# One layer of a graph network on one core: tile firsts looked up by one-hot products, x normalised by the scalar engine

## The reference

```
h    = relu(layernorm(x))                       # per node, no scale or offset
att  = sigmoid(h[src] @ Wa[:128] + h[dst] @ Wa[128:] + b_att)
msg  = (h[src] @ W_msg + b_msg) * att
agg  = segment_sum(msg, dst)
r, z, n = GRU gates of (agg, h);  h_new = (1 - z) * n + z * h
out  = x + gamma * (h_new - mean) * rsqrt(var + eps) + beta   # statistics over nodes
```

## Time and profile before

| | |
|---|---|
| median of 3 runs | 2263.29 us |
| the profiled execution | 2263.15 us, span 2261.4 us |
| PE, DVE, ACT, POOL busy | 91%, 89%, 88%, 74% of the span |
| last gather of the preparation starts on POOL | 162.91 us |
| first row gather (L774) | 164.16 us |
| `gate(0)` on ACT | 166.83 us |
| keys of half 1 copied, main gates on ACT | 191.39 us |

### The profile page before, as it was taken

One profiled execution on the slowest core, in us unless ns is written; L12 is line 12 of the kernel. 1 busy time (PEld: TensorE's weight loads), 2 busy tenths in 40 slices (PEclk: granted clock), 3 DMA queues, 4 the chain that ended last, 5 costly groups with the idle time before them and its releaser, 6 DMA issues.

```text
span 2261.4 us, 53825 instructions
## 1 busy us (share of the span) xinstructions
PE 2051.0 (91%) x18152; PEld 1986.7 (88%) x18152; DVE 2014.4 (89%) x4410; ACT 1995.5 (88%) x6980; POOL 1681.0 (74%) x1601
## 2 busy tenths in 40 slices
PE   3625999999999999999999999999999999999997
PEld 2514999999999999999999999999999999999986
DVE  5947899999999999999999999999999999999974
ACT  1359899999999999999999999999999999999943
POOL 5776777777777777777777777777777777777760
PEclk8765999999999999999999999999999999999998
DMA  9952222222223322222222222222223222323236
GB/s 148 268 150 64 56 60 60 60 61 62 61 60 61 63 60 63 62 63 57 61 62 62 61 61 60 63 59 61 63 60 63 59 62 59 63 60 64 59 112 224
DMA packets 171174, 171.65 MB, mean 76 GB/s; under 512 B 82872, under 2 KB 135146, under 8 KB 170770
## 3 DMA queue, kind: packets, MB, share of 16 engines
q0 software_dynamic: 50688, 104.63, 21.5%
q1 hardware_dynamic: 114564, 61.63, 10.8%
q10 hardware_dynamic: 5646, 1.93, 0.8%
HBM read 141.39 MB, written 26.66 MB: 74 GB/s over the span
## 4 chain that ended last, share of the span: by engine, by line
ACT 53%; PE 20%; DVE 15%; issue 8%; POOL 3%; DMA 2%; SPq 1%; DVEq 0%; ACTq 0%; POOLq 0%
ACT big L903 41%; PE ps L1444 11%; ACT gate_ring L899 9%; DVE big L1195 5%; PE ps L1429 3%; PE ps L1439 3%; POOL big L765 2%; DVE gate_ring L1179 2%; DMA big<-in_x_dram 1%; DVE key_hot L1165 1%; DVE lo_hot L1158 1%; PE ps L1450 1%; PE ps L1451 1%; ACT n_blk L908 1%; SPq L624 1%
## 5 line engine op out<-in xcount | busy, mean ns | idle before, releaser
L774 POOL DMA_INDIRECT row_ring<-node_table,set_idx x1480 | 1568.4, 1060 | 464.4 <-issue 331.5
L903 ACT ACTIVATE big<-set_score,big 128x128 f32<-128x128 f32 x5096 | 1632.6, 394 | 82.5 <-PE ps L1444 82.5
L1444 PE MATMUL ps<-big 128*128 128x128 f32 x10192 | 1445.6, 281 | 0.0
L1444 PEld LDWEIGHTS ps<-big 128*128 128x128 f32 x10192 | 1262.6, 193 | 0.0
L1195 DVE TENSOR_TENSOR big<-ps,big 128x784 f32<-128x784 f32 x832 | 803.3, 966 | 5.7 <-PE ps L1439 4.4
L1429 PE MATMUL ps<-gate_ring,row_ring 128*128 128x64 f32 x2960 | 535.3, 263 | 77.5 <-DVE gate_ring L1179 71.4
L1429 PEld LDWEIGHTS ps<-gate_ring,row_ring 128*128 128x128 f32 x2960 | 453.9, 194 | 124.2 <-DVE gate_ring L1179 110.0
L1179 DVE SCALAR_TENSOR_TENSOR gate_ring<-lane,set_rel,gate_ring 128x64 f32<-128x64 f32 x1480 | 414.5, 281 | 136.1 <-ACT gate_ring L899 130.5
L899 ACT ACTIVATE gate_ring<-set_win,row_ring 128x64 f32<-128x64 f32 x1480 | 492.2, 341 | 34.2 <-DMA row_ring<-node_table,set_idx 33.6
L1439 PE MATMUL ps<-key_hot,lo_hot 128*128 128x196 bf16 x3328 | 426.7, 251 | 28.7 <-DVE key_hot L1165 24.3
L1165 DVE TENSOR_TENSOR key_hot<-lane_key,set_key 128x1568 bf16<-128x1568 bf16 x416 | 402.7, 968 | 0.0
(11 more groups left out here) (124 smaller groups left out, 932.2 us busy)
## 6 DMA issues: line engine op xcount, KB each, us to landing
row_ring<-node_table,set_idx POOLq DMA_INDIRECT x1480
big<-in_x_dram SPq DMA_DIRECT2D x48, 256.0 KB, 5.7
h_blk<-hT_spill SPq DMA_DIRECT2D x97, 64.0 KB
node_table<-big SPq DMA_DIRECT2D x24, 258.0 KB
hT_spill<-big SPq DMA_DIRECT2D x24, 256.0 KB, 5.9
out_dram<-big SPq DMA_DIRECT2D x24, 256.0 KB
set_win<-dst_scores SPq DMA_DIRECT2D x148, 32.0 KB
set_score<-dst_scores SPq DMA_DIRECT2D x52, 64.0 KB
```

Of the source, the lines that this page charges most:

```text
L774: nc.gpsimd.indirect_dma_start(row_ring[:, t % ROWS_RING, :], None, table, bass.IndirectOffsetOnAxis(ap=set_idx[:, t // SET % 2, t % SET:t ...
L903: return nc.scalar.activation(a_buf[b % 2][:, h, :], set_score[:, b % 2, :], ACT.Sigmoid, bias=m_all[:, h, D:ROW])
L1444: return nc.tensor.matmul(ps[:, AM_BANK, 0:P], m_all[:, h, 0:D], a_buf[b % 2][:, h, :], start=h == 0, stop=h == HI - 1)
```

## The change

Three things are edited.

1. The search for tiles. `COARSE` becomes 125 and `FINE` 25. ACT loads all of dst (1.6 MB) into 125 partitions of 3200, and for each partition the first dst of the next one (124 elements); the DRAM table, its two element-wise copies, `find_rows` and the 26 gathers of L753 go. DVE cuts the first dst of each tile out of it (`find_starts`), makes for each half a mask of 125 x 1664 that is one where the query falls into the partition (two instructions), PE multiplies the mask with the 25 tile firsts and the number of the partition's first tile (13 products for a half, `read_starts`), and DVE counts in the product. That happens at c = 2 and 3, ahead of those passes' other work. POOL makes the line of 3328 queries by an `iota`.
2. The normalisation. z = x * rstd + shift on ACT with a scale and an offset for each row (four instructions for a chunk, in pass c for chunk c-1, behind the relu and the square root), with shift = -mean * rstd from DVE. DVE's four instructions of L1122 go. SP's load of x waits for z as before, which ACT now makes.
3. Places in the loop. `find_firsts` moves from c = 15 and 18 to c = 10 and 15, `sparse_windows` and ACT's cast from c = 5 to 8, the turning and copying of edges by three passes, the store of the sparse lists from c = 15 to 18.

```diff
-    COARSE = next(r for r in range(30, 0, -1) if TILES % r == 0)
+    COARSE = next(r for r in range(P, 0, -1) if TILES % r == 0)
...
@@ sync
-                if c == 15:
+                if c == 18:
                     sp.wait_ge(edges_kept, 8)
...
@@ gpsimd
+            nc.gpsimd.memset(row_next, float(NODES)).then_inc(q_line_made, 1)
+            nc.gpsimd.iota(starts[:, FINE:FINE + 1], [[0, 1]], base=0, channel_multiplier=FINE, ...
+            nc.gpsimd.iota(q_line, [[PAIR, QCOLS * P]], base=D0, channel_multiplier=0, ...
...
-            pool.wait_ge(starts_stored, 32)
-            pool.wait_ge(rows_found, 1)
-            for half in range(2):
-                rows = half_of(near, half, FINE)
-                for i, c in enumerate(HALVES[half]):
-                    nc.gpsimd.indirect_dma_start(rows[:, i, :], None, tile_starts, found(c)).then_inc(near_gathered[half], 16)
             for half in range(2):
                 rows = half_of(wins, half, P)
-                pool.wait_ge(near_gathered[half], 16 * len(HALVES[half]))
                 pool.wait_ge(tiles_found, half + 1)
@@ scalar
-                act.dma_start(coarse_i, ...), two act.dma_start into tile_starts
+            for rows in (slice(0, even_rows), slice(even_rows, COARSE)):
+                act.dma_start(dst_tiles[rows, :], tile_rows[rows, :]).then_inc(starts_loaded, 16)
+                for first, end in ((0, even_rows), (even_rows, COARSE - 1)):
+                    act.dma_start(next_i[first:end, :], tile_rows[first + 1:end + 1, 0:1]).then_inc(starts_loaded, 16)
...
+                if 0 <= c - 1 < CHUNKS:
+                    d, r = c - 1, (c - 1) % 2
+                    act.wait_ge(shift_done, d + 1)
+                    wait_reuse(act, z_turned, d - 1)
+                    for j, n in tiles_of(width_of(d)):
+                        last = nc.scalar.activation(zbuf[0:n, r, j, :], xbuf[0:n, d % 4, j, :], ACT.Identity,
+                                                    bias=shift[0:n, r, j:j + 1], scale=rstd[0:n, r, j:j + 1])
+                    last.then_inc(z_done, 1)
...
-                if c == 5:
+                if c == 8:
                     act.wait_ge(sparse_loaded, 64)
...
-                if 7 <= c < 17:
-                    keep_edges(c - 7)
+                if 10 <= c < 20:
+                    keep_edges(c - 10)
@@ vector
+            def find_starts():
+                dve.wait_ge(starts_loaded, 64)
+                dve.wait_ge(q_line_made, 3)
+                nc.vector.tensor_copy(starts[:, 0:FINE], dst_tiles.rearrange("r (f e) -> r f e", e=P)[:, :, 0])
+                link(nc.vector.tensor_copy(row_first, dst_tiles[:, 0:1]))
+                nc.vector.memset(row_first[0:1, :], -1.0)
+                link(nc.vector.tensor_copy(row_next[0:COARSE - 1, :], next_i[0:COARSE - 1, :]))
...
             def find_tiles(half):
-                dve.wait_ge(near_gathered[half], 16 * len(HALVES[half]))
-                cols = count_below(half, near[half], FINE)
+                cols, n = cols_of(half), len(HALVES[half])
+                queries, hot = q_line[:, half * QHALF * P:(half + 1) * QHALF * P], near[half][0:COARSE, :]
+                link(nc.vector.tensor_scalar(hot, queries, row_first, None, ALU.is_gt))
+                nc.vector.scalar_tensor_tensor(out=hot, in0=queries, scalar=row_next, in1=hot, op0=ALU.is_le, op1=ALU.mult
+                                               ).then_inc(tile_hots, 1)
+                dve.wait_ge(starts_read, half + 1)
+                rows = ps[:, 6 + half, 0:n * (FINE + 1)].rearrange("p (c f) -> p c f", f=FINE + 1)
+                below = grid(cmps, half, FINE)
+                link(nc.vector.tensor_tensor(below, rows[:, :, 0:FINE], at(q_at[:, cols], FINE), ALU.is_lt))
+                link(nc.vector.tensor_reduce(q_cnt[:, cols], below, AX_X, ALU.add))
                 link(nc.vector.tensor_scalar(q_tmp[:, cols], q_cnt[:, cols], -1.0, 0.0, ALU.add, ALU.max))
+                link(nc.vector.tensor_tensor(q_tile[:, cols], rows[:, :, FINE], q_tmp[:, cols], ALU.add))
                 nc.vector.tensor_copy(q_idx.bitcast(U32)[:, cols], q_tile[:, cols]).then_inc(tiles_found, 1)
...
-            find_rows()
             for c in range(CHUNKS + 3):
+                if c == 2:
+                    find_starts()
+                if c in (2, 3):
+                    find_tiles(c - 2)
                 if c < CHUNKS:
                     ...
+                    wait_reuse(dve, shift_done, c - 1)
...
-                    for j, n in tiles:
-                        last = nc.vector.tensor_scalar(zbuf[0:n, r, j, :], xbuf[0:n, d % 4, j, :],
-                                                       mv[0:n, r, j, 0:1], rstd[0:n, r, j:j + 1],
-                                                       ALU.subtract, ALU.mult)
-                    last.then_inc(z_done, 1)
+                    nc.vector.scalar_tensor_tensor(out=shift[:, r, 0:len(tiles)], in0=mv[:, r, 0:len(tiles), 0], scalar=-1.0,
+                                                   in1=rstd[:, r, 0:len(tiles)], op0=ALU.mult, op1=ALU.mult
+                                                   ).then_inc(shift_done, 1)
...
-                if c == 5:
+                if c == 8:
                     sparse_windows()
-                if c in (7, 11):
-                    find_tiles((c - 7) // 4)
-                if c in (15, 18):
-                    find_firsts((c - 15) // 3)
+                if c in (10, 15):
+                    find_firsts((c - 10) // 5)
@@ tensor
+            def read_starts(half):
+                pe.wait_ge(tile_hots, half + 1)
+                for i in range(len(HALVES[half])):
+                    last = nc.tensor.matmul(ps[:, 6 + half, i * (FINE + 1):(i + 1) * (FINE + 1)],
+                                            near[half][0:COARSE, i * P:(i + 1) * P], starts, start=True, stop=True)
+                last.then_inc(starts_read, 1)
...
             for c in range(CHUNKS + 2):
+                if c in (2, 3):
+                    read_starts(c - 2)
...
-                if 6 <= c < 16:
+                if 9 <= c < 19:
```

More of the change, by code:

```diff
@@ L159, in gnn_program @@
     assert SPARSE % SET == 0 and GROUPS % 2 == 0 and DENSE_AT + PARTS < STEPS_U + 4 and PARTS_AT + PARTS < STEPS_U and SETS > 2 and TILES % 16 == 5
+    assert QCOLS == 2 * QHALF and (FINE + 1) * QHALF <= 512 and FINE * P <= QCOLS * P
     assert B_FIRST < HI and first_tile(1) >= GATES_EARLY and ZEROED <= D0 and -(-STEPS // 5) <= WIN and all(
@@ L217, in gnn_program @@
         b_table = place(WIDE)
-        coarse_i = place(COARSE, 1).bitcast(I32)
-        coarse = place(COARSE, 1)
+        starts = place(FINE + 1, COARSE)
+        row_first = place(1, COARSE)
+        row_next = place(1, COARSE)
+        next_i = place(1, COARSE).bitcast(I32)
         assert spot[0] <= LN_AT + (HI - 10) * P
@@ L226, in gnn_program @@
         wins = [place(QHALF * P) for _ in range(2)]
+        dst_tiles = part(spot[0] - 2 * QHALF * P, FINE * P, COARSE).bitcast(I32)
         cmps = place(QHALF * P)
@@ L234, in gnn_program @@
         key_out = [place(QHALF * P) for _ in range(2)]
+        q_line = part(spot[0] - 2 * QHALF * P, 2 * QHALF * P, COARSE)
         b_turned = [place(P, rows) for rows in (B_FIRST, HI - B_FIRST)]
@@ L239, in gnn_program @@
         rstd = place(8).rearrange("p (b t) -> p b t", b=2)
+        shift = place(8).rearrange("p (b t) -> p b t", b=2)
         q_at = place(QCOLS)
-        q_row = place(QCOLS)
         q_tile = place(QCOLS)
@@ L350, in gnn_program @@
         rstd_done = sem("rstd_done")
+        shift_done = sem("shift_done")
         z_done = sem("z_done")
@@ L737, in _ @@
                                     pattern=[[1, P]], channel_multiplier=-1).then_inc(consts_made, 1)
+            nc.gpsimd.memset(row_next, float(NODES)).then_inc(q_line_made, 1)
+            nc.gpsimd.iota(starts[:, FINE:FINE + 1], [[0, 1]], base=0, channel_multiplier=FINE,
+                           allow_small_or_imprecise_dtypes=True).then_inc(q_line_made, 1)
+            nc.gpsimd.iota(q_line, [[PAIR, QCOLS * P]], base=D0, channel_multiplier=0,
+                           allow_small_or_imprecise_dtypes=True).then_inc(q_line_made, 1)
             def found(c):
@@ L836, in cast_lo @@
                 nc.scalar.copy(near[half][:, cols], near[half].bitcast(I32)[:, cols]).then_inc(lo_cast, 1)
-            with nc.allow_non_contiguous_dma(reason="one destination per tile of edges"):
-                act.dma_start(coarse_i, dst.rearrange("(o r e) -> o r e", o=1, r=COARSE)[:, :, 0]).then_inc(coarse_loaded, 16)
-                starts = dst.rearrange("(t e) -> t e", e=P)[:, 0]
-                stored = tile_starts.rearrange("r f -> (r f)")
-                act.dma_start(stored[TILES - 5:TILES].rearrange("(o n) -> o n", o=1),
-                              starts[TILES - 5:TILES].rearrange("(o n) -> o n", o=1)).then_inc(starts_stored, 16)
```

(9 more changed lines are left out.)

34 lines of the change are left out of this document (8 added, 26 removed).

## The result

Over 20 runs of each, the changed kernel takes 2266.93 us (2260.43 to 2273.82) and the kernel before 2264.31 us (2260.43 to 2267.84); the ratio is 1.0017 [1.001, 1.0025]. That is 3.9 us slower by the ratio, within 0.3%, where 8 us faster was forecast. The profiled execution took 2269.91 us, span 2268.2. The engines' shares of the whole span are within 2 points of those before (ACT 88 to 90%, DVE 89 to 88%).

The account below looks back on a forecast made before the run. POOL's gathers bound the kernel, the loop 10.6 us early; after the change the longer loop decides, gate at 158.6 against 166.83, so 2263.15 - 8.2 = 2254.95, 2255 us. Own range 2248 to 2262, all cases 2244 to 2268.

Parts of the forecast that it names:

- the sign of being wrong: Main stage: time from the first L899 (first row gate) to the end changes by more than 2 us.
- `gate(0)` possible at 158.6: First row gate on ACT: could start 27.0 us after the last score copy at 131.6, against 166.83 before.
- four take 1.2 ... so I add nothing for it: z on ACT: four instructions a chunk take 1.2 us, the scale by row beside the offset adds nothing.
- the store's ring: Loop: relu, root and z, SP's issue, landing of h span two passes; 3.05 to 4.15 us a pass.
- the ACT ring: Loop: relu, root and z on ACT, then PE's transposes before the next relu; 2.75 to 3.2 us a pass.
- 11.5 + 0.7 + 2.9 + 4.0 + 1.7 = 20.8: Start: dst load, `find_starts`, masks, products and counting in us; tiles of half 0 found at 20.8.
- The ten issues: Pass 4: ACT issues ten small DMAs ahead of the relu of chunk 3, taken as 7.5 us.
- C: Rival, loop: stores of h landing late set a slower pass; 2268 us at landing 5.9, 2274 at 6.6; chance 0.15.
- D: Rival, start: POOL's iota takes 19.6 us, all from pass 2 on 12 us later, 2267 us; chance 0.04.
- B: Rival, loop: as short as its lowest rows allow, 3.05 us a pass, 2245.6 us; chance 0.13.
- T: Loop: length of one pass with z on ACT, taken as 3.4 us, range 3.15 to 3.7.
- E: Rival: something else holds the main stage's start, under 2 of 8 us at the gate arrive, 2262 us; chance 0.06.

Follow-up runs that it names:

- b_zact: The kernel before the change with only z moved to ACT, scale and offset by row; 2265.22 us, ratio 1.0007 to the kernel before.
- a_zdve: The changed kernel with z given back to DVE, all else kept; 2257.51 us, ratio 0.9956 to the kernel before.
- a_noscale: The changed kernel with the scale by row left out of z on ACT, output wrong; 2264.39 us, ratio 0.9992 to the kernel before.
- a_twoprod2: The changed kernel with each half's 26 matmuls on PE done twice; 2282.14 us, ratio 1.0081 to the kernel before.
- reorg2: Changed kernel: z on DVE, ten small loads on POOL, dst behind two x chunks, sparse lists loaded at c = 3, look-up split and later; 2252.63 us, ratio 0.9944.
- a_xfirst: The changed kernel with the load of dst issued only after the first chunk of x landed; 2274.72 us, ratio 1.0032 to the kernel before.
- reorg: As reorg2, but the load of the sparse lists stays at c = 1; on the chip at 2630 us: 2610.16 us, ratio 0.9929.

## Why the prediction was wrong

*What bound the kernel before*: right. POOL's gathers held `gate(0)` and the loop had 10.6 us of slack; `b_zact` ate 5.6 of it unseen. *That after the change the loop decides and not POOL*: right, the first row gather is 17 us ahead of the gate. *That the time follows the gate*: in direction only. The gate is 3.5 us later, the profiled execution 6.8 longer, so 3.3 us came in behind the gate, more than the 2 us that I had named as the sign of being wrong. That 2263.15 + 3.5 comes near the median of 2266.93 is luck in part: over ten profiles what lies behind the gate differs by 10.3 us, more than the gate's own 3.5. Over the nine edited kernels gate and ratio do go together, to within 6 us.

What failed is the size of the loop: its pass with z on ACT, and its start. I had `gate(0)` possible at 158.6 and it came at 170.31, 11.7 us late, in three parts.

1. **"four take 1.2 ... so I add nothing for it"**, the price of z on ACT. I took it from instructions with one operand by row at the same size, and for the second had only a row of 512 columns with both (0.70), with no partner that had one. z took 1.64 us: 0.44 more in each pass, and in both rings. With 1.64 in my formula the store's ring gives 3.6 and the ACT ring up to 3.6 us, where I had 3.4; the passes that PE ended took 3.5. From the relu of chunk 3 to the last one it was 88.3 us against 83.2: 5.1 too short. `a_noscale` shows 3.3 us of these for the second operand, where PE's pace may have a share; the other 1.8 stay open. At the gate it is 6.1 us at most, and `a_zdve` shows 10.3 for z's place. Giving z back to DVE turns the sign (ratio 0.9956); the second operand alone doesn't (0.9992, with 1 in its interval).
2. **"11.5 + 0.7 + 2.9 + 4.0 + 1.7 = 20.8"**, the start. Loads and first statistics took until 15.85, 4.4 us more (inside my bounds of 9 to 16, at their end), and the products 5.75 in place of 4.0. With DVE and PE each standing for the other, the relu of chunk 3 was at 51.0 and not 45.7: 5.3. I had seen that DVE loses its early wait for x as a gain; in the trace the wait came back, at 12.57, behind 1.4 MB of dst. `a_twoprod2` and `reorg2` show that this stretch is on the path; `a_xfirst` shows that it isn't mended by the order of two loads. The ten issues took 6.2 us where I had 7.5 and made the error smaller by that much.
3. From the last relu on it took 1.3 us more than from rows of before: 0.9 until the last score copy (its wait for PE was 3.29 us, and 2.39 before), 0.4 behind it.

The rivals: C (stores that land at 5.9 us or later, a gate at 172.1) has the right time, 2268, by luck: the landing was 4.4, my own figure, and the late start made up the time that C gave to late stores. Its ring is real, a fifth of the chain, but opening it gave 1.3 us at the gate. The 2.6 us that I had worked out from the Trainium skill, DMA: Bandwidth & Descriptors, section Anatomy of one DMA, and set aside, rest on a fit to transfers that GpSimd issues, where SP issues these; no store landed in under 3.1 us. D fell: the iota took 2.90 us. B fell with T at 3.5. E fell: what was late was the change's own work. The range over all cases, 2244 to 2268, held the median; the forecast's own, 2248 to 2262, didn't, and what held it was the rivals' width and not a mechanism that came true.

## What to carry to other kernels

Moving work from a full engine to an idle one pays only if the new place isn't between two steps of a ring: price it as latency in the chain relu, z, transposes, not as busy time. Slack that one part of a change is to use can't be used by another part as well; test each alone on the kernel before and on the one after. An operand more on an instruction is a term of its own, and where the trace has no pair of rows that differ in it alone, its bounds have to be as wide as one more fixed cost for every instruction. And a variant that leaves a term out prices it only where nothing else moved: compare stage by stage, as the passes here, before the gate's whole difference is put down to the edit.

## What was not expected of the hardware

- 26 matmuls of 125x26 f32 took 5.75 us in the changed kernel, 0.22 us each and hardly less than 0.24 for 128x130, and 3.27 us (0.126 each) for the second half in `reorg2`, whose first half took 5.58. The windows inside a slow and a fast stretch (columns as in the earlier trace rows) give a granted clock of 1.00, the 2.4 GHz level, for both; in `a_twoprod2` a window inside the second half's products has 0.50, the 1.2 GHz level (in this order):

```profile
22.00:25.00 3.00, 3.00 (x15) 3.00 (x15) 0.00 (x0) 0.00 (x0) 0.00 (x0) 1.00 1.04 208
```

```profile
42.00:45.00 3.00, 3.00 (x27) 3.00 (x28) 1.98 (x10) 0.30 (x1) 2.18 (x3) 1.00 0.28 69
```

```profile
42.00:45.00 3.00, 3.00 (x16) 3.00 (x15) 0.00 (x0) 0.00 (x0) 2.09 (x4) 0.50 0.17 44
```

  15 and 27 matmuls in 3 us at one recorded clock, and 16 at half of it: the slow early stretch has the pace of 0.50. Transposes there take 1.11 us too (30.07 in the changed kernel), as they do later at 0.50. Why the record has 1.00 for them stays open. The same second half took 5.58 us in the changed kernel and 3.40 in `a_noscale`, each behind a gap on PE and 2.6 us of work. So early PE work has two prices that the edit doesn't set; who prices it takes the slow row, and who compares variants looks at which they got.
- One iota of 3328 numbers took 2.90 us, 0.9 ns a number; the two rows of before have 5.9 and 1.5 ns a number.
- On one chip the kernel before takes 2629.84 us in place of 2264 to 2266. In the one trace of it whose chain I followed, that of `reorg`, there are stretches of 11.7 to 19.3 us that the profile puts down to another core or an unknown queue. The kernel with doubled products is faster than the one before there (0.9974) and slower on the other chip (1.0081).
